# First-layer weights kept as two parts in memory, second-layer weights kept on chip and picked by a register

## Chip, cores and metric

The kernel runs on one core of one Trainium2 chip. The metric is the device time in microseconds (us) of one execution, the median of three.

## What is computed

The reference is one transformer block over `x` of shape (8, 512, 128), all in float32: a linear attention with 16 heads of 64, a residual and a layer norm, then a mixture of 8 experts of which each token takes 2, another residual and a second layer norm. The part that the change is about is the expert part:

```python
logits = einsum('bsd,ed->bse', x, gate_w); probs = softmax(logits)
topk_probs, topk_idx = top_k(probs, 2)
h = gelu(einsum('bsd,fed,bske->bskf', x, w1, onehot) + b1[topk_idx])   # 128 -> 512
y = einsum('bskf,def,bske->bskd', h, w2, onehot) + b2[topk_idx]       # 512 -> 128
x = layernorm(x + sum_k(y * topk_probs))
```

There are 4096 tokens, so 8192 pairs of a token and an expert.

## The kernel before, in words

**Attention.** It runs batch by batch (8 batches `b` of 512 tokens), in `attention(b)` on each engine. TensorE (PE) does keys, queries, a Gram matrix of the inputs with the keys, the norms and the output. Products that need float32 accuracy are made by the helper `three` (L432 to L436): each operand is split into a high part in the type fp32r and the rest, a low part, and three fp32r matmuls are added up. The high part is a copy by ScalarE (ACT, helper `hi`, L666), the low part a subtraction by VectorE (DVE, helper `lo`, L819) or GpSimd (POOL). Near the end of a batch PE runs: half of the queries, two of four tiles of the Gram matrix's first half (`gram(0, (0, 1))`), `norms`, the other two tiles, the second half `gram(1, ...)`, and `mix`. `gram(1)` waits for `n_step` (L563), that is for DVE's instruction of L1116, which reads the norms out of the same PSUM bank. On ACT that place has, in order, the queries' evictions, `first_norm(p)` (L752), the split of the next batch's `xT` (L757) and the eviction of the Gram matrix `gm` (L762). On DVE it has `means` and `scale_logits` (L1111, L1112) and then L1116.

**Experts.** The routed rows are written to a table in memory (`xs`), sorted by expert, and worked off in NBLK = 39 blocks of 256 rows of one expert each, n = 0 to 38. Which expert and which rows a block has is known only at run time; it stands in a table `tabi`, of which the first EARLY = 17 blocks are ready at the end of the attention and the other 22 later (they wait for the last batch's rows). Each engine runs its own list in order:

- SyncE (SP) loads the rows of block n (`load_rows`, L319) and its weights (`load_weights`, L315): it reads the table's entry into a register (`value_load`), and starts a DMA whose address depends on it. One block's weights are one DMA of 578 KB: w1 (128 x 512), b1, w2 (4 x 128 x 128) and b2, 4624 bytes on each of 128 partitions, into one of 6 slots. The loads of block n wait until block n - 6 is finished. Between them SP clears the ends of the experts' regions (`clear_end`, two at each of n = 11 to 14), at n = 17 waits for the last batch's scattered rows (L356 to L360), and from n = 31 on starts the fetches of finished results (`fetch`, L331).
- PE runs, in its iteration n (L651): `turn_rows(n)` (two transposes of the rows), `first_layer(n - 1)` (four float32 matmuls of 256 columns, L639), `second_layer(n - 2)` (eight float32 matmuls of 128 columns, L648). A float32 matmul is two passes in the trace, so that L639 has 8 entries and L648 has 16 in each block.
- ACT copies the transposed rows out of PSUM (L803, L667 in the trace), and does the four gelus with b1 as bias (L794).
- DVE adds b2 (L1136) and scales and adds the rows (L1139) in `result(n - 2)`. After it, in the same list, come the last batch's layer norm and routing (n = 0 to 6), the making of the late table (n = 7 to 11) and, from n = 31 on, statistics of the final layer norm (`last_means`, `last_chain`, at the n of STAT_AT and CHAIN_AT, L57 and L58). `last_means(g)` waits until the fetch of group g has landed.
- POOL scatters the last batch's rows (L395, one piece each at n = 5 to 12) and stores each block's results (L419, two indirect DMAs a block).

What is left of the order: `turn_rows(n)` waits for ACT's copy of the block before (`e_Th`, one PSUM bank up to n = 8, two from then on), and `first_layer(n)` for the copy of its own rows.

```python
for n in range(NBLK + 2):                 # TensorE, L651
    if n < NBLK: turn_rows(n)
    if 1 <= n <= NBLK: first_layer(n - 1)
    if n >= 2: second_layer(n - 2)
```

Of the kernel before, what the change touches and what calls it, by code (L numbers as in the profile page):

```python
# [27 lines left out]
ds = bass.ds  # L28
# [40 lines left out]
KT_SLOTS = 4  # L69
W_ROW = F + FC + FC * D + D  # L70

# [41 lines left out]
def program(nc, x, xT, wqkvT, wf, bf, wout, bout, gwT, w12, consts, out):  # L113
    ctx = ExitStack()
    with ctx:
# [16 lines left out]
        def con(name, rows=P):  # L132
# [5 lines left out]
        wq_hi, wq_lo = sb("wq_hi", [P, HD], F32R), sb("wq_lo", [P, HD], F32R)  # L138
        wk_hi, wk_lo = sb("wk_hi", [P, HD], F32R), sb("wk_lo", [P, HD], F32R)
        vo = sb("vo", [P, H * D])  # L140
        xT_hi, xT_lo = sb("xT_hi", [P, S], F32R), sb("xT_lo", [P, S], F32R)
# [63 lines left out]
        past_l = [qn_space[0:1, a * 704:(a + 1) * 704] for a in range(2)]  # L205
        rows_T = r_rest[:, :]
# [4 lines left out]
        w_raw = [xT_raw[:, u * W_ROW:(u + 1) * W_ROW] for u in range(3)] + [  # L211
            x_raw[:, :, :].rearrange("p c d -> p (c d)")[:, u * W_ROW:(u + 1) * W_ROW] for u in range(SLOTS - 3)]
        w2_raw = [w[:, F + FC:W_ROW - D].rearrange("p (c n) -> p c n", c=FC) for w in w_raw]
        b2_bc = [w[:, None, W_ROW - D:].broadcast_to([P, 2, D]) for w in w_raw]
        x1_space = x1[:, :, :].rearrange("p c d -> p (c d)")
        pair = [space[:, i * TILES * TOPK * D:(i + 1) * TILES * TOPK * D].rearrange("p (t k d) -> p t k d", k=TOPK, d=D)
                for space, i in ((x1_space, 0), (x1_space, 1), (x1_space, 2), (x1_space, 3), (qn_space, 0), (qn_space, 1), (x1_space, 0), (x1_space, 1))]
# [16 lines left out]
        def before(n):  # L234
# [18 lines left out]
        e_x, e_w, e_out = ([sem(f"{n}{u}") for u in range(ROW_SLOTS)] for n in ("e_x", "e_w", "e_out"))  # L253
        e_T, e_Th, e_up, e_gelu, e_down, e_y0, e_y1, e_y = (
            sem(n) for n in ("e_T", "e_Th", "e_up", "e_gelu", "e_down", "e_y0", "e_y1", "e_y"))
        in_xr0, in_fold_q, in_fold_v, tab_step = (sem(n) for n in ("in_xr0", "in_fold_q", "in_fold_v", "tab_step"))
# [35 lines left out]
        def _(sp):  # L292
# [20 lines left out]
            sp.dma_start(xs[NOWHERE:NOWHERE + BLK, :].rearrange("(p f) c -> p f c", p=P), zeros[:, :, :]).then_inc(filled, 16)  # L313

            def load_weights(n):  # L315
                expert = sp.value_load(tabi[0:1, 0, n:n + 1], min_val=0, max_val=E - 1)
                sp.dma_start(w_raw[n % SLOTS], w12[ds(expert, 1), :, :].rearrange("a p n -> (a p) n")).then_inc(e_w[n % SLOTS], 16)

            def load_rows(n):  # L319
                first = sp.value_load(tabi[0:1, 1, n:n + 1], min_val=0, max_val=NOWHERE)  # L320
                sp.dma_start(xrow[n % ROW_SLOTS], xs[ds(first, BLK), :].rearrange("(c p) d -> p c d", p=P)).then_inc(e_x[n % ROW_SLOTS], 16)

            sp.wait_ge(table, 2)
            sp.wait_ge(scattered, 16 * TILES * TOPK * SAFE)
# [104 lines left out]
        def _(pe):  # L429
# [190 lines left out]
            def turn_rows(n):  # L620
                pe.wait_ge(e_x[n % ROW_SLOTS], 16 * (n // ROW_SLOTS) + 16)
                if n == 0:
                    pe.wait_ge(qn_done, CH * B)
                else:
                    pe.wait_ge(e_Th, before(n))
                for c in range(2):
                    last = pe.transpose(psX2[bank_of(n)][:, c * P:(c + 1) * P], xrow[n % ROW_SLOTS][:, c, 0:D], con("ident"))
                last.then_inc(e_T, 1)

            def first_layer(n):  # L630
                v = n % 2
                u = n % SLOTS
                pe.wait_ge(e_Th, n + 1)
                pe.wait_ge(e_w[u], 16 * (n // SLOTS) + 16)
# [6 lines left out]
            def second_layer(n):  # L641
                v = n % 2
                pe.wait_ge(e_gelu, FC * (n + 1))
                if n >= 1:
                    pe.wait_ge(e_y0, before(n))
                for t in range(2):
                    for c in range(FC):
                        last = mm(psY2[bank_of(n)][:, t, :], hT[v][:, c, t * P:(t + 1) * P], w2_raw[n % SLOTS][:, c, :], start=c == 0, stop=c == FC - 1)  # L648
                last.then_inc(e_down, 1)

            for n in range(NBLK + 2):  # L651
                if n < NBLK:
                    turn_rows(n)
                if n == 0:
                    logits(B - 1)
                if 1 <= n <= NBLK:
                    first_layer(n - 1)
                if n >= 2:
                    second_layer(n - 2)
                if n == 6:  # L660
                    ranks(B - 1)
# [3 lines left out]
        def _(act):  # L665
# [30 lines left out]
            def first_norm(p):  # L696
                act.wait_ge(ln_step, LN_STEPS * (p + 1))
                for j in range(TILES):
# [88 lines left out]
            def gelu(n):  # L787
                v, u = n % 2, n % SLOTS
                act.wait_ge(e_w[u], 16 * (n // SLOTS) + 16)
                for c in range(FC):  # L790
                    act.wait_ge(e_up, FC * n + c // 2 * 2 + 2)
                    if c == 0 and n >= 2:
                        act.wait_ge(e_down, n - 1)
                    act.activation(hT[v][:, c, :], psH[v][:, c, :], ACT.Gelu_apprx_tanh,  # L794
                                   bias=w_raw[u][:, F + c:F + c + 1]).then_inc(e_gelu, 1)

            for n in range(NBLK + 1):
                if n < NBLK:
# [3 lines left out]
                    v = n % 2  # L802
                    hi(rows_T[:, v * BLK:(v + 1) * BLK], psX2[bank_of(n)], scale=2.0).then_inc(e_Th, 1)  # L803
                if n >= 1:
# [13 lines left out]
        def _(dve):  # L818
# [227 lines left out]
            def attention(b):  # L1046
# [172 lines left out]
```

## Time and profile before

| what | value |
|---|---|
| three executions | 472.32, 473.69, 474.63 us; median 473.69 |
| the profiled execution | 474.31 us, of which the span from first to last instruction is 472.5 |
| busy: PE, DVE, ACT, POOL | 437.2, 300.6, 273.1, 162.2 us |
| mean granted PE clock | 0.983 |

Columns of the rows below: in the timeline, start and length in us, engine, line of the kernel, operation, out<-in by the program's names, shape, xcount, and in brackets the engine's idle time just before and what ended it. PEld is PE's weight load, SPq an instruction in SP's own queue. The names are those of the memory: the weights' slots lie in `xT_raw` and `x_raw`, the blocks' rows in `kT` and `rn`, the hidden layer and the results in `q_act`, the final groups in `x` and `qn`. Entries of the same kind that follow each other are merged into one row, and its length is then that of them all, overlaps and drain included.

### The profile page before, as it was taken

How to read it: one execution, taken by the hardware profiler on the slowest of the kernel's cores; microseconds unless marked ns; L12 is line 12 of the kernel's file. 1: busy time of each engine (PE TensorE's matmuls, PEld its weight loads, DVE VectorE, ACT ScalarE, POOL GpSimd, SP SyncE). 2: the span in 40 equal slices, each digit the busy share in tenths (PEclk: the TensorE clock that was granted, in tenths of full speed). 3: DMA queues.
4: the chain of work that ended last, by engine and by line, in shares of the span. 5: the costliest groups of instructions: out<-in, count | busy, mean ns of one | idle time of the engine just before them, and what ended most of it. 6: DMA issues, size and time to landing. Idle time of an engine off the chain costs nothing.

```text
span 472.5 us, 8134 instructions
## 1 busy us (share of the span) xinstructions
PE 437.2 (93%) x2608; PEld 343.4 (73%) x2608; DVE 300.6 (64%) x896; ACT 273.1 (58%) x531; POOL 162.2 (34%) x164
## 2 busy tenths in 40 slices
PE   4888999999999999999999998799999999999940
PEld 4666776676677677667677674499998999999930
DVE  2654865976976967967967967743563222245784
ACT  2763655665666665665666562278555555555672
POOL 2101101131332233233143133165777545555540
PEclk9999999999999999999999999999999999999995
DMA  8920000000000000000000000598895998799343
GB/s 222 336 70 0 3 0 1 0 19 6 26 23 1 25 23 1 23 25 6 19 24 13 12 25 23 171 318 234 235 276 167 321 286 238 232 337 311 122 134 112
DMA packets 34442, 52.19 MB, mean 110 GB/s; under 512 B 4943, under 2 KB 24788, under 8 KB 34272
## 3 DMA queue, kind: packets, MB, share of 16 engines
q1 hardware_dynamic: 25296, 40.75, 28.4%
q0 software_dynamic: 4544, 8.54, 5.1%
q10 hardware_dynamic: 4560, 2.39, 1.7%
q8 instruction: 21, 0.34, 0.3%
q14 instruction: 21, 0.17, 0.1%
HBM read 39.82 MB, written 12.75 MB: 111 GB/s over the span
## 4 chain that ended last, share of the span: by engine, by line
PE 82%; DVE 6%; DMA 4%; issue 3%; SPq 2%; POOL 2%; ACT 1%; POOLq 0%; DVEq 0%; ACTq 0%
PE psA L639 13%; PE psO L531 11%; PE psG L648 8%; PE psA L434 6%; PE psA L436 6%; PE psA L435 6%; PE psA L510 6%; PE psS L648 5%; PE psG L434 4%; PE psG L551 3%; PE psG L435 3%; PE psG L436 3%; PE psA L578 3%; PE psG L522 3%; DMA x_raw<-x 1%
## 5 line engine op out<-in xcount | busy, mean ns | idle before, releaser
L395 POOL DMA_INDIRECT expert_rows<-rows,pos x64 | 62.5, 977 | 116.7 <-DVE pos L1025 91.1
L419 POOL DMA_INDIRECT expert_results<-q_act,kT x56 | 55.3, 987 | 41.6 <-DVE q_act L1139 30.5
L531 PE MATMUL psO<-qn,mixed 128*128 128x512 f32 x128 | 65.8, 599 | 0.4 <-DVE qn L1056 0.4
L667 ACT ACTIVATE kT<-psA,bf_col 128x512 f32<-128x512 f32 x64 | 44.0, 687 | 37.0 <-PE psA L436 36.7
L667 ACT ACTIVATE q_act<-psA,bf_col 128x512 f32<-128x512 f32 x64 | 43.9, 690 | 26.4 <-PE psA L436 26.3
L1056 DVE TENSOR_TENSOR qn<-q_act,psG 128x512 f32<-128x512 f32 x64 | 43.0, 681 | 5.0 <-PE psG L522 5.0
L820 DVE TENSOR_TENSOR k_lo<-psA,k_hi 128x512 fp32r<-128x512 f32 x64 | 43.7, 686 | 3.5 <-ACT k_hi L667 2.8
L510 PEld LDWEIGHTS psA<-cst,kT 128*128 128x128 f32 x256 | 30.8, 140 | 16.2 <-ACT kT L667 8.3
L794 ACT ACTIVATE q_act<-psA,xT_raw 128x256 f32<-128x256 f32 x84 | 34.6, 471 | 11.8 <-PE psA L639 11.1
L639 PE MATMUL psA<-r_rest,xT_raw 128*128 128x256 f32 x168 | 41.3, 391 | 0.0
L434 PE MATMUL psA<-xT_hi,wk_hi 128*128 128x512 f32 x64 | 41.0, 641 | 0.0
L510 PE MATMUL psA<-cst,kT 128*128 128x128 f32 x256 | 38.7, 274 | 2.4 <-DVE k_lo L820 1.4
L667 ACT ACTIVATE k_hi<-psA 128x512 fp32r<-128x512 f32 x64 | 38.1, 596 | 2.0 <-PE psA L510 2.0
L1068 DVE TENSOR_REDUCE ksum<-kT 128x2 f32<-128x1024 f32 x32 | 38.7, 1210 | 0.0
L794 ACT ACTIVATE q_act<-psA,x_raw 128x256 f32<-128x256 f32 x72 | 29.7, 471 | 8.4 <-PE psA L639 8.0
L639 PE MATMUL psA<-r_rest,x_raw 128*128 128x256 f32 x144 | 34.1, 379 | 0.0
L639 PEld LDWEIGHTS psA<-r_rest,xT_raw 128*128 128x128 f32 x168 | 31.2, 196 | 3.6
L648 PEld LDWEIGHTS psG<-xT_raw,q_act 128*128 128x128 f32 x256 | 31.0, 192 | 1.4 <-ACT q_act L794 0.6
L386 POOL TENSOR_TENSOR xT_lo<-xT_raw,xT_hi 128x512 fp32r<-128x512 f32 x8 | 10.3, 1284 | 63.3 <-ACT xT_hi L667 63.3
L648 PE MATMUL psG<-xT_raw,q_act 128*128 128x128 f32 x256 | 31.3, 275 | 0.4 <-ACT q_act L794 0.4
L386 POOL TENSOR_TENSOR x_lo<-x_raw,x_hi 128x512 fp32r<-128x512 f32 x8 | 10.3, 1292 | 59.5 <-ACT x_hi L667 59.5
L667 ACT ACTIVATE gm<-psG 128x512 f32<-128x512 f32 x16 | 9.6, 597 | 34.1 <-PE psG L436 34.1
(180 smaller groups left out, 915.8 us busy)
## 6 DMA issues: line engine op xcount, KB each, us to landing
xT_raw<-w SPq DMA_DIRECT2D x21, 578.0 KB, 4.7
x_raw<-w SPq DMA_DIRECT2D x18, 578.0 KB
kT<-expert_rows SPq DMA_DIRECT2D x28, 132.0 KB, 4.6
x<-expert_results SPq DMA_DIRECT2D x5, 512.0 KB, 6.4
xT_raw<-xT SPq DMA_DIRECT2D x1, 1792.0 KB, 10.4
q_act<-wqkvT SPq DMA_DIRECT2D x3, 512.0 KB, 6.9
rn<-expert_rows SPq DMA_DIRECT2D x11, 132.0 KB, 3.7
out<-x ACTq DMA_DIRECT2D x5, 256.0 KB, 2.3
```

The source lines that it names most:

```text
L395: pool.indirect_dma_start(xs, bass.IndirectOffsetOnAxis(ap=pos[:, j, k:k + 1], axis=0), rows[:, j, k, :], None).then_inc(scattered if o < ...
L419: pool.indirect_dma_start(ys, bass.IndirectOffsetOnAxis(ap=xrow[r][:, c, D:D + 1].bitcast(I32), axis=0), yrow[u][:, c, :], None, bounds_ch ...
L434: mm(outp, a_hi, b_hi, start=start, stop=False)
L435: mm(outp, a_hi, b_lo, start=False, stop=False)
L510: last = pe.transpose(bankA[2 + c % 2][:, at], kT[:, (CH * b + c) % KT_SLOTS, at], con("ident"))
L531: mm(psO[:, :], mixed[:, c, :], qn[:, c % 4, :], start=c == 0, stop=c == CH - 1).then_inc(o_pe, 1)
L639: mm(psH[v][:, c, :], w_raw[u][:, c * P:(c + 1) * P], rows_T[:, at], start=True, stop=True).then_inc(e_up, 1)
L648: last = mm(psY2[bank_of(n)][:, t, :], hT[v][:, c, t * P:(t + 1) * P], w2_raw[n % SLOTS][:, c, :], start=c == 0, stop=c == FC - 1)
L667: return act.activation(out_, in_, func, **kw)
L794: act.activation(hT[v][:, c, :], psH[v][:, c, :], ACT.Gelu_apprx_tanh, bias=w_raw[u][:, F + c:F + c + 1]).then_inc(e_gelu, 1)
L820: return dve.tensor_tensor(out_, full_, hi_.bitcast(F32), ALU.subtract)
L1056: dve.tensor_tensor(qn[:, c % 4, :], q_act[:, c, :], psG[:, c % 2, :], ALU.mult).then_inc(qn_done, 1)
```

## The change

The first layer is made by `three` instead of by float32 matmuls: 12 fp32r matmuls of 256 columns a block instead of 4 float32 ones. For this w1 is split once for each of the 8 experts, during attention batches 1 to 4 (two experts each, `SPLIT_AT`), by ACT and DVE, and written back to memory as `w1s` (high and low part side by side). SP loads w1's two parts for each block (512 KB) and b1 and b2 by two small DMAs. w2 of all experts is loaded once (2 MB) and stays on chip; PE reads the block's expert into a register (`choose`) and the matmuls of the second layer take w2 at an address that depends on it. The rows' low part is a new instruction of DVE at the head of each iteration, and PE waits for it (`e_Tl`) where it waited for ACT's copy (`e_Th`).

```diff
-W_ROW = F + FC + FC * D + D
+W_ROW = FC + D
+W1_SLOTS = 8
+SPLIT_AT = {1: (0, 1), 2: (2, 3), 3: (4, 5), 4: (6, 7)}
...
+        w1s = nc.dram_tensor("expert_weights", [E, P, 2 * F], F32, kind="Internal").ap()
...
+            for half in range(2):
+                if half:
+                    sp.wait_ge(w1_l, E // 2)
+                sp.dma_start(w1_raw, w12[4 * half:4 * half + 4, :, 0:F].rearrange("e p f -> p e f")).then_inc(in_w1[half], 16)
+                for ex in range(4 * half, 4 * half + 4):
+                    sp.wait_ge(w1_l, ex + 1)
+                    sp.dma_start(w1s[ex, :, :], w1_split[ex % 2][:, :].bitcast(F32)).then_inc(w1_out[ex % 2], 16)
+            sp.wait_ge(x_l, B)
+            sp.wait_ge(x_h, B)
+            sp.dma_start(w2_all.rearrange("p (e n) -> p e n", e=E), w12[:, :, F + FC:F + FC + FC * D].rearrange("e p n -> p e n")).then_inc(w2_in, 16)
...
             def load_weights(n):
                 expert = sp.value_load(tabi[0:1, 0, n:n + 1], min_val=0, max_val=E - 1)
-                sp.dma_start(w_raw[n % SLOTS], w12[ds(expert, 1), :, :].rearrange("a p n -> (a p) n")).then_inc(e_w[n % SLOTS], 16)
+                sp.dma_start(w1_slot[n % W1_SLOTS].bitcast(F32), w1s[ds(expert, 1), :, :].rearrange("a p n -> (a p) n")).then_inc(e_w[n % W1_SLOTS], 16)
+                for cols, part in ((slice(0, FC), slice(F, F + FC)), (slice(FC, W_ROW), slice(F + FC + FC * D, F + FC + FC * D + D))):
+                    sp.dma_start(b_raw[n % SLOTS][:, cols], w12[ds(expert, 1), :, part].rearrange("a p n -> (a p) n")).then_inc(e_b[n % SLOTS], 16)
...
# TensorE, turn_rows: waits for e_Tl, not e_Th
+            def choose(n):
+                if n == 0:
+                    pe.wait_ge(w2_in, 16)
+                if n in (0, EARLY):
+                    pe.wait_ge(table, 2 if n == 0 else 4)
+                return pe.value_load(tabi[0:1, 0, n:n + 1], min_val=0, max_val=E - 1)
...
             def first_layer(n):
-                pe.wait_ge(e_Th, n + 1)
+                pe.wait_ge(e_Tl, n + 1)
                 for c in range(FC):
-                    mm(psH[v][:, c, :], w_raw[u][:, c * P:(c + 1) * P], rows_T[:, at], start=True, stop=True).then_inc(e_up, 1)
+                    three(psH[v][:, c, :], w1_slot[u][:, c * P:(c + 1) * P], w1_slot[u][:, F + c * P:F + (c + 1) * P],
+                          xT_hi[:, at], xT_lo[:, at]).then_inc(e_up, 1)
...
             def second_layer(n, expert):
-                        last = mm(psY2[bank_of(n)][:, t, :], hT[v][:, c, t * P:(t + 1) * P], w2_raw[n % SLOTS][:, c, :], ...)
+                        last = mm(psY2[bank_of(n)][:, t, :], hT[v][:, c, t * P:(t + 1) * P], w2_all[:, ds(expert * (FC * D) + c * D, D)], ...)
...
             for n in range(NBLK + 2):
                 if n >= 2:
-                    second_layer(n - 2)
+                    second_layer(n - 2, expert)
+                if 1 <= n <= NBLK:
+                    expert = choose(n - 1)
...
# ScalarE, attention(b), after the split of the next xT and before gm
+                    for ex in SPLIT_AT.get(b, ()):
+                        act.wait_ge(in_w1[ex // 4], 16)
+                        if ex >= 2:
+                            act.wait_ge(w1_out[ex % 2], 16 * (ex // 2))
+                        hi(w1_split[ex % 2][:, 0:F], w1_raw[:, ex % 4, :]).then_inc(w1_h, 1)
...
# VectorE, attention(b), after scale_logits and before L1116
+                for ex in SPLIT_AT.get(b, ()):
+                    dve.wait_ge(w1_h, ex + 1)
+                    lo(w1_split[ex % 2][:, F:], w1_raw[:, ex % 4, :], w1_split[ex % 2][:, 0:F]).then_inc(w1_l, 1)
...
# VectorE, experts, at the head of iteration n
+                if n < NBLK:
+                    at = slice(n % 2 * BLK, (n % 2 + 1) * BLK)
+                    dve.wait_ge(e_Th, n + 1)
+                    dve.scalar_tensor_tensor(xT_lo[:, at], psX2[bank_of(n)], 2.0, xT_hi[:, at].bitcast(F32), ALU.mult, ALU.subtract).then_inc(e_Tl, 1)
```

## Rows read from the trace of the kernel before

**Rows 1.** The page: busy time, and DMA busy share in 40 slices.

```profile
PE 437.2 (93%) x2608; PEld 343.4 (73%) x2608; DVE 300.6 (64%) x896; ACT 273.1 (58%) x531; POOL 162.2 (34%) x164
...
DMA  8920000000000000000000000598895998799343
```

**Rows 2.** The page: the chain that ended last, shares of the span by line.

```profile
PE psA L639 13%; PE psO L531 11%; PE psG L648 8%; PE psA L434 6%; PE psA L436 6%; PE psA L435 6%; PE psA L510 6%; PE psS L648 5%; PE psG L434 4%; PE psG L551 3%; PE psG L435 3%; PE psG L436 3%; PE psA L578 3%; PE psG L522 3%; DMA x_raw<-x 1%
```

**Rows 3.** Timeline of one block of the steady expert stretch.

```profile
377.06 0.38 PE L627 MATMUL psG<-cst,kT 128*128 128x128 f32 x2
...
377.26 0.42 DVE L1136 TENSOR_TENSOR q_act<-psS,x_raw 128x256 f32<-128x256 f32 x1 [2.66 <-PE psS L648]
377.28 1.89 PE L639 MATMUL psA<-r_rest,xT_raw 128*128 128x256 f32 x8
...
377.72 0.61 DVE L1139 SCALAR_TENSOR_TENSOR q_act<-q_act,rn 128x128 f32<-128x128 f32 x2
...
379.01 1.95 PE L648 MATMUL psG<-xT_raw,q_act 128*128 128x128 f32 x16
...
380.79 0.38 PE L627 MATMUL psO<-cst,kT 128*128 128x128 f32 x2
```

**Rows 4.** Timeline of attention batch 1, around L1116 and the Gram matrix.

```profile
73.53 0.64 ACT L667 ACTIVATE xT_hi<-xT_raw 128x512 fp32r<-128x512 f32 x1
...
74.24 1.28 POOL L386 TENSOR_TENSOR xT_lo<-xT_raw,xT_hi 128x512 fp32r<-128x512 f32 x1 [24.43 <-ACT xT_hi L667]
...
74.35 0.69 DVE L1116 TENSOR_SCALAR rn<-psG 128x512 f32<-128x512 f32 x1 [2.02 <-PE psG L551]
...
75.50 0.39 PE L436 MATMUL psG<-k_hi,x_lo 128*128 128x512 f32 x1
...
75.72 0.39 PE L434 MATMUL psG<-k_hi,x_hi 128*128 128x512 f32 x1
...
75.92 0.60 ACT L667 ACTIVATE gm<-psG 128x512 f32<-128x512 f32 x1 [1.76 <-PE psG L436]
```

**Rows 5.** Groups of instructions (busy us, mean ns | idle before): the nearest to the new splits.

```profile
L820 DVE TENSOR_TENSOR k_lo<-psA,k_hi 128x512 fp32r<-128x512 f32 x64 | 43.7, 686 | 3.5 <-ACT k_hi L667 2.8
...
L1146 DVE TENSOR_TENSOR x<-x 128x512 f32<-128x512 f32 x4 | 2.7, 685 | 0.0
```

**Rows 6.** SP's queue at the start of the experts; the page's DMA issues.

```profile
302.09 0.34 SPq L317 DMA_DIRECT2D xT_raw<-w  x1
...
304.35 0.34 SPq L317 DMA_DIRECT2D xT_raw<-w  x1
...
xT_raw<-w SPq DMA_DIRECT2D x21, 578.0 KB, 4.7
```

**Rows 7.** Instructions of L316 on SP (ns min/median/max): a register load.

```profile
L316 SPq TENSOR_LOAD <-tabi x39: 262/274/563, 299.1 to 434.4; - x39
L316 SPq FUSED_REGOPS  x39: 152/152/165, 299.4 to 434.7; - x39
```

**Rows 8.** Timeline of SP's queue with two clears between loads.

```profile
330.83 1.55 SPq L341 DMA_DIRECT2D expert_rows<-zeros  x2
...
333.15 0.41 SPq L321 DMA_DIRECT2D kT<-expert_rows  x1
```

**Rows 9.** Timeline around block 17: its row load and PE's first use.

```profile
363.47 0.38 SPq L321 DMA_DIRECT2D rn<-expert_rows  x1
...
365.81 0.44 PE L627 MATMUL psO<-cst,rn 128*128 128x128 f32 x2 [0.45 <-DMA rn<-expert_rows]
```

**Rows 10.** Timeline of the late stretch: statistics on DVE, and one fetch.

```profile
423.03 0.68 DVE L1146 TENSOR_TENSOR x<-x 128x512 f32<-128x512 f32 x1
...
424.73 0.38 DVE L1153 BATCH_NORM_AGGREGATE mv<-stats 128x2 f32<-128x6 f32 x4
...
432.66 0.33 SPq L336 DMA_DIRECT2D qn<-expert_results  x1
...
437.96 0.69 DVE L1146 TENSOR_TENSOR x<-x 128x512 f32<-128x512 f32 x1
```

More of the change, by code:

```diff
@@ L139, in program @@
         wk_hi, wk_lo = sb("wk_hi", [P, HD], F32R), sb("wk_lo", [P, HD], F32R)
+        w1_split = [sb(f"w1_split{i}", [P, 2 * F], F32R) for i in range(2)]
         vo = sb("vo", [P, H * D])
@@ L210, in program @@
                 for space, fit in ((kT_space, 7), (rn_space, ROW_SLOTS - 7)) for u in range(fit)]
[L211 to L214, printed above, removed]
+        b_raw = [xT_raw[:, u * W_ROW:(u + 1) * W_ROW] for u in range(SLOTS)]
+        b2_bc = [b[:, None, FC:].broadcast_to([P, 2, D]) for b in b_raw]
+        w1_slot = [space[:, u, :] for space in (k_hi, k_lo) for u in range(W1_SLOTS // 2)]
+        w2_all = x_raw[:, :, :].rearrange("p c d -> p (c d)")
         x1_space = x1[:, :, :].rearrange("p c d -> p (c d)")
+        w1_raw = x1_space[:, 4 * F:8 * F].rearrange("p (e f) -> p e f", f=F)
         pair = [space[:, i * TILES * TOPK * D:(i + 1) * TILES * TOPK * D].rearrange("p (t k d) -> p t k d", k=TOPK, d=D)
@@ L253, in program @@
         e_x, e_w, e_out = ([sem(f"{n}{u}") for u in range(ROW_SLOTS)] for n in ("e_x", "e_w", "e_out"))
-        e_T, e_Th, e_up, e_gelu, e_down, e_y0, e_y1, e_y = (
-            sem(n) for n in ("e_T", "e_Th", "e_up", "e_gelu", "e_down", "e_y0", "e_y1", "e_y"))
+        e_T, e_Th, e_Tl, e_up, e_gelu, e_down, e_y0, e_y1, e_y = (
+            sem(n) for n in ("e_T", "e_Th", "e_Tl", "e_up", "e_gelu", "e_down", "e_y0", "e_y1", "e_y"))
+        in_w1 = [sem(f"in_w1_{i}") for i in range(2)]
+        w1_h, w1_l, w2_in = (sem(n) for n in ("w1_h", "w1_l", "w2_in"))
+        w1_out = [sem(f"w1_out{i}") for i in range(2)]
+        e_b = [sem(f"e_b{u}") for u in range(SLOTS)]
         in_xr0, in_fold_q, in_fold_v, tab_step = (sem(n) for n in ("in_xr0", "in_fold_q", "in_fold_v", "tab_step"))
@@ L321, in load_rows @@
                 sp.dma_start(xrow[n % ROW_SLOTS], xs[ds(first, BLK), :].rearrange("(c p) d -> p c d", p=P)).then_inc(e_x[n % ROW_SLOTS], 16)
+            for which in w1_out:
+                sp.wait_ge(which, 16 * E // 2)
             sp.wait_ge(table, 2)
@@ L624, in turn_rows @@
                 else:
-                    pe.wait_ge(e_Th, before(n))
+                    pe.wait_ge(e_Tl, before(n))
                 for c in range(2):
@@ L628, in turn_rows @@
                 last.then_inc(e_T, 1)
+            def choose(n):
[4 more added lines that the diff above has]
+                return pe.value_load(tabi[0:1, 0, n:n + 1], min_val=0, max_val=E - 1)
             def first_layer(n):
-                v = n % 2
-                u = n % SLOTS
-                pe.wait_ge(e_Th, n + 1)
-                pe.wait_ge(e_w[u], 16 * (n // SLOTS) + 16)
+                v, u = n % 2, n % W1_SLOTS
+                pe.wait_ge(e_w[u], 16 * (n // W1_SLOTS) + 16)
+                pe.wait_ge(e_Tl, n + 1)
                 if n >= 2:
@@ L638, in first_layer, with second_layer @@
                 for c in range(FC):
-                    mm(psH[v][:, c, :], w_raw[u][:, c * P:(c + 1) * P], rows_T[:, at], start=True, stop=True).then_inc(e_up, 1)
-            def second_layer(n):
+                    three(psH[v][:, c, :], w1_slot[u][:, c * P:(c + 1) * P], w1_slot[u][:, F + c * P:F + (c + 1) * P],
+                          xT_hi[:, at], xT_lo[:, at]).then_inc(e_up, 1)
+            def second_layer(n, expert):
                 v = n % 2
@@ L647, in second_layer @@
                     for c in range(FC):
-                        last = mm(psY2[bank_of(n)][:, t, :], hT[v][:, c, t * P:(t + 1) * P], w2_raw[n % SLOTS][:, c, :], start=c == 0, stop=c == FC - 1)
+                        last = mm(psY2[bank_of(n)][:, t, :], hT[v][:, c, t * P:(t + 1) * P], w2_all[:, ds(expert * (FC * D) + c * D, D)], start=c == 0, stop=c == FC - 1)
                 last.then_inc(e_down, 1)
@@ L697, in first_norm @@
                 act.wait_ge(ln_step, LN_STEPS * (p + 1))
+                if p == 4:
+                    act.wait_ge(w1_l, E)
                 for j in range(TILES):
@@ L788, in gelu @@
                 v, u = n % 2, n % SLOTS
-                act.wait_ge(e_w[u], 16 * (n // SLOTS) + 16)
+                act.wait_ge(e_b[u], 32 * (n // SLOTS) + 32)
                 for c in range(FC):
@@ L802, in _ @@
                     v = n % 2
-                    hi(rows_T[:, v * BLK:(v + 1) * BLK], psX2[bank_of(n)], scale=2.0).then_inc(e_Th, 1)
+                    hi(xT_hi[:, v * BLK:(v + 1) * BLK], psX2[bank_of(n)], scale=2.0).then_inc(e_Th, 1)
                 if n >= 1:
```

3 lines of the change are left out of this document (1 added, 2 removed).

## The prediction

> **What bounds the kernel now.** I began with the page: PE is busy 93% of the span, the others 64% or less [rows 1], and the chain that ended last runs through PE's lines in both stages, L639 and L648 in the experts and L531 and L434 to L436 in the attention [rows 2]. So a pass saved on PE is time saved, unless something else is close behind it. The timeline of one block shows how close. PE's period is 3.73 us (377.06 to 380.79): 0.22 for the transposes, 1.73 for the first layer's eight passes, 1.78 for the second layer's sixteen [rows 3]. In that time DVE needs 1.07 us for a block's result (377.26 to 378.33) and then waits for PE. DMA engines are busy 0.7 to 0.9 in most of the expert stage [rows 1]; the bytes per block stay the same (578 KB), so I leave them at nothing, with the prefetch of several blocks as cover. The close one is SP, which is not on the chain: its loads for a block follow each other at 2.26 us when it waits for nothing [rows 6].
>
> **First layer on PE.** Removed: 8 passes of 256 columns, 1.73 us. Added: 12 fp32r passes of 256 columns. The nearest rows are fp32r passes of 512 columns, 0.22 to 0.23 us apart (75.50 to 75.72) [rows 4]; half is 0.115. The weight load must fit under a pass: in L648 a load and a pass come every 0.111 us (1.78 / 16) [rows 3], so 0.115 is not below what it allows. Lower end 0.111; upper end 0.23, if an fp32r load could not be hidden under a shorter pass. I take 0.115, as L648's pace is the nearer row: 1.38 us, a saving of 0.35, and a PE period of 3.38 us.
>
> **SP.** A block now has four DMAs instead of two. A pair of register load and DMA costs 1.13 us (2.26 / 2). The two new DMAs use a register that is already loaded. Each costs at least its own 0.34 [rows 6], and at most 1.13 less the load (0.274) and the register operation (0.152) of rows 7, about 0.7. I take 0.52, the middle, as both ends are the same instruction with and without its address work. SP's period becomes 2.26 + 1.04 = 3.30 us (2.94 to 3.66), beside PE's 3.38: nothing is left to catch up with. Where SP has more to do, PE now waits. That is at the clears of n = 11 to 14, at 2.3 us for each pair (330.83 to 333.15) [rows 8], 9.2 us in all.
>
> **The early blocks, up to block 17.** Before, the weights of block 1 are issued at 302.09 [rows 6]. Now it is about 303.1 (block 0's two small DMAs precede them), so those of block 16 go out at 303.1 + 15 x 3.30 + 9.2 = 361.8 and land 4.7 later [rows 6], at 366.5. Block 16's rows are one SP step earlier (about 360.7) and arrive near 364 to 365; with block 15's first layer and block 14's second behind their transposes (3.4 us) PE reaches block 17 at about 367.4, not at 365.81 [rows 9]. Block 17's own rows are no earlier either: they were issued at 363.47, after the scatter [rows 9], and SP gets there at about 364. The whole early gain (17 x 0.35 = 6 us) is lost and **1.6 us** are added. If SP's step were 2.94, this would be 17 x 0.35 less what the scatter's chain holds back, some 2 us gained; at 3.66, 7 us lost.
>
> **The late blocks, 17 to 38.** 21 periods x 0.35 = **-7.3 us**. Against it stands DVE. The new low part of block n + 1 is at the head of DVE's iteration, behind whatever the iteration before left, and PE's first layer waits for it; before, PE waited only for ACT. Its price: 128x256 from PSUM, as L1136, 0.42 [rows 3], 0.46 with its gap. From n = 31 on a statistics iteration costs 2.1 us (423.03 to 425.11) [rows 10] besides the result's 1.07: with the 0.46 together 3.63, above 3.38. Three such iterations in a row cost 0.8; the norm chain and the next ones about as much again. The fetch issued at 432.66 was used at 437.96 [rows 10], 5.3 us later with no wait. Now two more small DMAs precede its issue (1.04) and four blocks between come 4 x 0.35 sooner, so DVE waits some 2.4 us at n = 37 with block 38's low part behind it, part of which the queues absorb. Together I give back **3.0 us** (1 to 5). The tail after the last transposes has one first layer in it, **-0.3**.
>
> **Attention, batches 1 to 4.** Two splits each on ACT, 0.64 us like xT_hi [rows 4], and two subtractions on DVE, 0.69 each [rows 5]. On ACT they fit: it stood idle 1.76 us before gm, and takes 1.3. On DVE they do not. ACT is free at 74.17, the splits end at 74.8 and 75.5, the second subtraction at about 76.2, and only then comes L1116, which ran at 74.35: 1.85 us late, done at 76.9. gram(1) waits for it, and its first pass started at 75.72 [rows 4]: PE stands 1.2 us, 1.35 with the wake-up. POOL and SP have nothing behind it. Later in the batch DVE's reciprocal and the norms shift by as much as PE, so it is not paid twice. 4 x 1.35 = **+5.4 us** (0, if PE had slack that I do not see, to 7). The stores of w1s and w2's load run while DMA is idle [rows 1] and cost nothing.
>
> By a rule of the Trainium skill (SBUF — State Buffer, Who interferes with whom) a VectorE instruction with two SBUF inputs contends with a GpSimd instruction that reads SBUF. The new subtractions are of that kind.
>
> The trace has such an instruction of DVE only where POOL does no arithmetic (L1146, 685 ns) [rows 5]. POOL's xT_lo runs from 74.24 to 75.52 [rows 4], over the first subtraction's start at 74.9. If it must wait, 0.65 us a batch are added.
>
> **Register on PE.** `choose` costs PE's own queue a load and a register operation, 0.43 us by SP's [rows 7], and each of 8 matmuls may need address work. The queue runs ahead of the array, so I put it at nothing; the cover is the work queued in front. Not hidden, it would be 0.43 and more a block.
>
> **Sum.** 5.4 + 1.6 - 7.3 + 3.0 - 0.3 = +2.4, or 2.5 with the small DMAs at the start. On the profiled execution (474.31, span 472.5 and 1.8 around it) that is 476.8; it lies 0.6 above the median, so for the median 473.7 + 2.5 = **476.2 us**.
>
> **Rivals.** A measurement of this kernel tells 0.5% (2.4 us) from no change: below 471.3 is faster, above 476.1 slower.
>
> *A, the forecast.* Own range 471 to 480. Chance 0.42 (0.04 faster, 0.20 same, 0.18 slower).
>
> *B, the saving comes through.* It decides at SP's new DMAs: at 0.4 or less each its step is below 3.1 and PE keeps its own pace. Early -2, late -7.3 + 2, tail -0.3, attention +4: -3.6, 470.1. For it: both added DMAs skip the register load. Against it: address work remains. Chance 0.28 (0.26 faster).
>
> *C, SP sets the pace.* At 0.7 each its step is 3.66. Early +7, late 21 x (3.66 - 3.73) = -1.5, the fetches' own time on SP +1.5, attention +5.4: +12.4, 486. Chance 0.10.
>
> *D, three passes cost what two did or more.* Passes of 0.144 make the saving zero, and the sum without its -7.3 and without most of the 3.0 is 481; at 0.23 a block is 1.03 longer, 473.7 + 5.4 + 39 x 1.03 = 519. Against it is L648's pace. Chance 0.02. That is also the case in which the change doesn't do what it says.
>
> *E, PE's queue does not run ahead.* Register load (0.43) and the address work of 8 matmuls (0.05 each at the least) then show in each block, 0.8 us, 0.45 more than the saving: 473.7 + 5.4 + 39 x 0.45 = 497. Nothing in the trace shows a matmul with such an address. Chance 0.10.
>
> *F, the subtractions wait for POOL.* 4 x 0.65 = 2.6 on top: 478.8. Chance 0.08, as no row shows it. By the rule of the Trainium skill named above it would be certain.
>
> **How the numbers follow.** The forecast is A's. The range 467.5 to 486 takes in A, B, C and F with SP's and DVE's bounds, and leaves out D, E and the thin ends, 0.2. Faster 0.26 + 0.04 = 0.30; same 0.20 + 0.02 = 0.22; slower 0.18 + 0.10 + 0.02 + 0.10 + 0.08 = 0.48.
>
> **What the changed profile would show.** Right: L434 to L436 with 256 columns every 0.115 us; L1116 about 1.9 us later against the norms and PE idle 1.3 us before gram(1) in batches 1 to 4; four SP DMAs a block, 3.3 us apart, and PE waiting for `expert_rows` loads around blocks 12 to 17; block 17 at or after 366 plus the attention's 5; a late pace of 3.38 with waits of PE for DVE's low part from n = 31 on. Wrong: an SP step under 3.1, no PE idle at gram(1), or PE idle in every block between second layer and transposes, which would be the register.

## The result, and the profile after

The changed kernel takes **489.12 us** (median of 4, 487.52 to 493.09) where the kernel before takes 474.16 (472.32 to 474.96) on the same chip: 1.034 times as long, 95% interval 1.030 to 1.039. The forecast was 476.2 with a range to 486. The profiled execution has a span of 485.8 us, 13.3 over the 472.5 of before. Seven of the eighteen runs below fell on chips where the kernel before itself takes 490 to 491 us, so each is read by its ratio to the kernel before beside it; most of those seven were made again on a chip where that takes 475, but not `e6_pool_after` and `s3_before_pieces`. A ratio leaves out executions more than 1.5% above the fastest of the same kernel, which are two of `e1_split_later` alone. Brackets behind a ratio are its 95% interval.

I cut both traces at the same places: the start of the first expert block's transposes, of block 17's, and of block 38's, the last. Below, a period of PE is the time from one block's first transpose to the next one's, and a step of SP the time from the issue of one block's rows to that of the next.

| stretch | before | after | difference | forecast |
|---|---|---|---|---|
| to block 0 (the attention) | 302.1 | 309.4 | +7.3 | +5.4 |
| block 0 to 17 | 63.7 | 70.1 | +6.4 | +1.6 |
| block 17 to 38 | 78.4 | 79.6 | +1.2 | -4.3 |
| block 38 to the end | 28.3 | 26.7 | -1.6 | -0.3 |
| sum | 472.5 | 485.8 | +13.3 | +2.4 |

The page after, parts 1, 2 and 4 (they answer to [rows 1, 2]):

```profile
PE 434.1 (89%) x2764; PEld 345.0 (71%) x2764; DVE 322.2 (66%) x943; ACT 275.0 (57%) x539; POOL 162.0 (33%) x164
...
PE   4979998998998998999999998799968999979950
...
PE 56%; SPq 15%; DVE 11%; issue 7%; DMA 6%; ACT 3%; POOL 1%; POOLq 0%; DVEq 0%; ACTq 0%
PE psO L554 10%; PE psA L457 6%; PE psA L459 6%; PE psA L458 6%; PE psA L533 5%; SPq L338 4%; PE psA L601 3%; PE psG L457 3%; PE psG L545 3%; PE psG L679 2%; SPq L341 2%; PE psG L458 2%; PE psG L459 2%; PE psS L679 2%; SPq L342 2%
```

PE's busy time fell by only 3 us, although 39 first layers are shorter, in part because some of it ran at half clock (below). And SP's queue, with 2% of the chain before, now holds 15% of it, with the two small DMAs (L338) as its largest line. What PE waited for (us in total, times, longest):

```profile
PE psG L650 <- DMA kT<-expert_rows: 7.8, 5, 2.3
PE psG L457 <- DVE rn L1159: 6.1, 4, 1.6
PE psO L650 <- DMA kT<-expert_rows: 3.7, 3, 2.5
...
PE psG L650 <- DMA rn<-expert_rows: 0.7, 1, 0.7
```

Two waits have come up: for the row loads that SP issues (12.2 us in nine; before, one of 0.5 us at block 17), and for DVE's L1159 (none for L1116, as it was before). The timeline of a late block, which answers to [rows 3]; where PE starts late, the row names what released it:

```profile
389.87 0.38 PE L650 MATMUL psG<-cst,kT 128*128 128x128 f32 x2
...
390.05 1.46 SPq L342 DMA_DIRECT2D kT<-expert_rows  x1
...
390.45 0.28 PE L457 MATMUL psA<-xT_hi,k_hi 128*128 128x256 f32 x1
...
390.56 0.28 PE L458 MATMUL psA<-xT_lo,k_hi 128*128 128x256 f32 x1
...
391.06 0.41 DVE L1208 SCALAR_TENSOR_TENSOR xT_lo<-psG,xT_hi 128x256 fp32r<-128x256 f32 x1
...
391.52 1.95 PE L679 MATMUL psG<-x_raw,q_act 128*128 x16
...
392.27 0.33 SPq L336 DMA_DIRECT2D k_lo<-expert_weights  x1
392.80 0.85 SPq L338 DMA_DIRECT2D xT_raw<-w  x2
...
394.43 0.33 PE L650 MATMUL psO<-cst,kT 128*128 128x128 f32 x1 [0.96 <-DMA kT<-expert_rows]
```

The passes are 0.12 us apart and the two layers follow each other without a gap: PE's period is 3.43 us where nothing is late. Here something is: one SP issue (L342) took 1.46 us instead of 0.38, and PE stands 0.96 us at the rows of the block after. SP's queue over the clears, which answers to [rows 8]:

```profile
345.10 1.57 SPq L364 DMA_DIRECT2D expert_rows<-zeros  x2
347.50 0.41 SPq L342 DMA_DIRECT2D kT<-expert_rows  x1
348.83 0.35 SPq L336 DMA_DIRECT2D k_hi<-expert_weights  x1
349.38 0.85 SPq L338 DMA_DIRECT2D xT_raw<-w  x2
350.99 1.47 SPq L364 DMA_DIRECT2D expert_rows<-zeros  x2
353.21 0.41 SPq L342 DMA_DIRECT2D kT<-expert_rows  x1
```

A step with clears takes 5.71 us (347.50 to 353.21), and PE's blocks 11 to 14 are 5.93, 6.12, 5.76 and 5.03 us apart. In the attention, batch 1, which answers to [rows 4]:

```profile
73.75 1.16 ACT L700 ACTIVATE w_split<-x 128x512 fp32r<-128x512 f32 x2
...
73.95 1.29 POOL L409 TENSOR_TENSOR xT_lo<-xT_raw,xT_hi 128x512 fp32r<-128x512 f32 x1 [24.42 <-ACT xT_hi L700]
...
74.42 1.96 DVE L860 TENSOR_TENSOR w_split<-x,w_split 128x512 fp32r<-128x512 f32 x2 [2.39 <-ACT w_split L700]
...
76.31 0.68 DVE L1159 TENSOR_SCALAR rn<-psG 128x512 f32<-128x512 f32 x1
...
77.04 0.50 PE L457 MATMUL psG<-k_hi,x_hi 128*128 128x512 f32 x1 [1.44 <-DVE rn L1159]
```

The two subtractions take 1.96 us together, L1159 starts at 76.31 where L1116 did at 74.35, and PE's second Gram half at 77.04 instead of 75.72. The batch itself began 0.28 us earlier here (PE's first key matmul at 45.95, before at 46.23), so that within the batch L1159 is 2.24 us later. Last, three stretches of the experts (us; busy time and instructions of each engine, then granted clock, DMA share, GB/s):

```profile
313.30:320.10 6.80, 6.07 (x30) 5.78 (x29) 3.84 (x22) 3.82 (x10) 5.26 (x6) 0.50 0.93 241
368.00:371.40 3.40, 3.40 (x19) 3.40 (x17) 0.42 (x1) 2.03 (x5) 2.33 (x3) 0.50 0.80 246
436.20:439.60 3.40, 3.40 (x19) 3.40 (x18) 1.15 (x7) 1.87 (x5) 1.27 (x2) 0.50 0.96 289
```

The granted clock is 0.50, the lower level of 1.2 GHz, for 13.6 us; in the kernel before for only 3.4 us between its first and its last expert block (305.8 to 309.2). The last two stretches follow waits of PE for rows.

### The profile page after: what moved, and what is told of

It is laid out like the page before. It is cut to its first block, busy times and chain, and to the rows that moved or that the text cites. A ratio compares the mean times of both kernels' runs of the same rounds, so it can differ in the third digit from the quotient of the medians.

```text
span 485.8 us, 9037 instructions
## 1 busy us (share of the span) xinstructions
PE 434.1 (89%) x2764; PEld 345.0 (71%) x2764; DVE 322.2 (66%) x943; ACT 275.0 (57%) x539; POOL 162.0 (33%) x164
## 4 chain that ended last, share of the span: by engine, by line
PE 56%; SPq 15%; DVE 11%; issue 7%; DMA 6%; ACT 3%; POOL 1%; POOLq 0%; DVEq 0%; ACTq 0%
PE psO L554 10%; PE psA L457 6%; PE psA L459 6%; PE psA L458 6%; PE psA L533 5%; SPq L338 4%; PE psA L601 3%; PE psG L457 3%; PE psG L545 3%; PE psG L679 2%; SPq L341 2%; PE psG L458 2%; PE psG L459 2%; PE psS L679 2%; SPq L342 2%
## 5 line engine op out<-in xcount | busy, mean ns | idle before, releaser
L834 ACT ACTIVATE q_act<-psA,xT_raw 128x256 f32<-128x256 f32 x156 | 61.7, 476 | 17.5 <-PE psA L459 17.2
L679 PE MATMUL psG<-x_raw,q_act 128*128 x384 | 48.7, 281 | 0.2 <-ACT q_act L834 0.2
L679 PEld LDWEIGHTS psG<-x_raw,q_act 128*128 128x128 f32 x384 | 47.0, 199 | 0.5 <-issue 0.4
L1179 DVE TENSOR_TENSOR q_act<-psG,xT_raw 128x256 f32<-128x256 f32 x24 | 10.2, 424 | 38.9 <-PE psG L679 38.6
L457 PE MATMUL psG<-k_hi,x_hi 128*128 128x512 f32 x64 | 26.4, 413 | 7.9 <-DVE rn L1159 6.1
L409 POOL TENSOR_TENSOR x_lo<-x_raw,x_hi 128x512 fp32r<-128x512 f32 x8 | 10.4, 1295 | 66.6 <-ACT x_hi L700 66.6
L409 POOL TENSOR_TENSOR xT_lo<-xT_raw,xT_hi 128x512 fp32r<-128x512 f32 x8 | 10.3, 1287 | 63.1 <-ACT xT_hi L700 63.1
L679 PE MATMUL psS<-x_raw,q_act 128*128 x240 | 29.2, 275 | 0.0
L457 PE MATMUL psA<-xT_hi,wq_hi 128*128 128x512 f32 x64 | 28.5, 446 | 0.0
```

Source lines behind the costliest of these rows:

```text
L457: mm(outp, a_hi, b_hi, start=start, stop=False)
```

## The experiments

In kernels with more lines the same instruction has a higher number: L650 of the changed kernel is L655 in e2, e3, r2 and r4, and L633 in r3.

**My theory:** (a) the subtractions stand in front of L1159 and make PE wait, more than forecast because POOL holds them up; (b) SP's step with two more issues leaves no lead over PE, so its clears, fetches and long issues reach PE. **Rivals:** the low part on DVE, PE's own passes or the register set the experts' pace; or it is memory traffic and not issue time.

### The subtractions on DVE

`e1_split_later`:

```
-                for ex in SPLIT_AT.get(b, ()):  (ahead of L1159)
+                    (the same three lines behind the reciprocals of L1163)
```

> Edit: the two subtractions of w1's low parts are taken from in front of DVE's L1159 (the norms) and put behind the two reciprocals of L1163, where DVE waits some 1.9 us a batch for ACT. Theory (the subtractions delay L1159, and PE's second Gram half waits for it, 4 x 1.84 us, the stall of 1.9 to 2.0 us seen in batches 1 to 4): all of the 7.3 us of the attention come back, batch periods of 34.2 to 34.5 us, about 481.8 us. Rival (the splits cost through ACT, POOL or DMA, wherever DVE does its part): at most 2 us come back, over 487.

Measured: 485.67 us (478.46 to 487.03), 1.015 [1.004, 1.026], the ratio from 478.46 and 485.44 alone. DVE in batch 1:

```profile
74.75 0.69 DVE L1156 TENSOR_SCALAR rn<-psG 128x512 f32<-128x512 f32 x1 [2.03 <-PE psG L574]
75.48 3.37 DVE L1160 RECIPROCAL rn<-rn 128x256 f32<-128x256 f32 x2
...
78.76 1.22 DVE L860 TENSOR_TENSOR w_split<-x,w_split 128x512 fp32r<-128x512 f32 x2
```

Both subtractions take 1.22 us with POOL done, PE's wait for L1159 is gone, and the periods of batches 1 to 4 (from PE's first key matmul to that of the next batch) are 34.22, 34.53, 34.53 and 34.83 (before 34.22, 34.51, 34.56, 34.53; after 35.93, 36.25, 36.40, 36.68). So the attention's loss is this one place: block 0 starts at 303.0 instead of 309.4. The total doesn't follow, though: the profiled run, of 485.90 us, took 153.2 us from block 0 to 38 instead of 149.6, with 9 SP issues over half a microsecond, 8.4 us of excess. The runs lie 8.6 us apart. That the rest of the 7.3 us is lost in SP's queue is likely, not shown by this run alone; between e2 and e3 below, where SP has two DMAs a block, the same edit gives 6.9 us.

`e6_pool_after` (POOL's L409 in batches 1 to 4):

```
                 pool.wait_ge(xT_h, b + 2)
+                if b in SPLIT_AT:
+                    pool.wait_ge(w1_l, SPLIT_AT[b][-1] + 1)
```

> Edit: in batches 1 to 4 POOL's xT_lo waits until DVE has done both subtractions of w1. Theory (the first subtraction takes 1.3 us instead of 0.68 because POOL reads memory at the same time): both subtractions 0.68 us, L1159 0.6 us earlier, 4 x 0.6 = 2.4 us less in the attention, batch periods of 35.4 to 36.0 us, 486.5 us in all. Rival (the first of the two is slow by itself, by its form or ACT's write just before it): still 1.3 us, and no change or slightly slower.

Measured: 508.28 us on a chip where the kernel before takes 489.95, 1.040 [1.033, 1.047]; the total says nothing without the changed kernel beside it, but the attention's periods can be read: the kernels that have the changed kernel's attention agree in them to 0.1 us on all chips. All eight subtractions (ns min/median/max), and batch 1:

```profile
L862 DVE TENSOR_TENSOR w_split<-x,w_split x8: 684/689/694, 75.9 to 183.9; 128x512 fp32r<-128x512 f32 x8
```
```profile
75.92 1.29 DVE L862 TENSOR_TENSOR w_split<-x,w_split 128x512 fp32r<-128x512 f32 x2 [2.39 <-ACT w_split L702]
...
77.36 1.28 POOL L409 TENSOR_TENSOR xT_lo<-xT_raw,xT_hi 128x512 fp32r<-128x512 f32 x1 [26.35 <-DVE w_split L862]
```

In the changed kernel the same row read 676/1020/1375. Periods of 35.29, 35.55, 35.78 and 36.04, 2.6 us less in all. The contention is shown: a subtraction that starts under POOL's takes 1.3 us (1.96 less 0.68 in batch 1; 1.36 to 1.38 by its own record in each of the four batches, 0.69 here), and POOL itself loses nothing (1.29 and 1.28 us).

### SP's two small DMAs

`e2_one_load`:

```
+W1_ROW = 2 * F + W_ROW          (b1 and b2 stored beside w1's two parts)
-                for cols, part in (...): sp.dma_start(b_raw[...])
-        w1_slot: 8 of 2 * F columns
+        w1_slot: 6 of W1_ROW columns, b_raw = w[:, 2 * F:]
```

> Edit: the biases are stored beside w1's two parts in memory, so that one DMA brings 1156 columns a block where three DMAs did; six slots of weights instead of eight. Theory (SP's step of 3.3 us and its lack of a lead cost the early and the late blocks): SP step 2.26 us, waits of PE for expert_rows gone or under 2 us in all, the span from the first transposes to the last 13 to 14 us shorter (early 8, late 5 to 6), about 475.5 us. Rival (DVE's low part and the clock set the experts' pace, SP only follows): less than 4 us come back, over 485.

Measured: 476.11 us (473.67 to 478.13), 1.001 [0.998, 1.004]. As expected, SP's step is 2.26; block 0 to 38 took 134.7 us instead of 149.6. One long wait of PE for rows is left, 2.6 us behind block 16, where SP waits 8.5 us for POOL's scatter of the last batch; all such waits together are 4.0 us, where under 2 was expected. Not expected: the first batch ended 4.1 us later (its last products began at 48.2, not 44.1). I put it down to the biases' loads, which stand in front of other work in the queue at the start; but single profiles of kernels without them show late first batches too (50.9 in r3), so it isn't shown.

`e7_before_small` and again `r3_before_small`, the kernel before with the loads alone:

```
+                for cols, part in (...): sp.dma_start(spare[:, n % SLOTS, cols], w12[...])
```

> The kernel before, with two small DMAs of the biases added behind each block's weights (into a tile that nothing reads), and nothing else of the change. Theory (SP's added issues cost by themselves): SP's step from 2.26 to 3.3 us and more with long issues among them, early blocks 3 to 6 us later, late ones 0 to 2, about 479 us (476 to 483). Rival (the small DMAs only hurt together with a shorter PE period): within 1.5 us of the kernel before.

> As e7_before_small (the kernel before, with two small DMAs of the biases added to each block's loads). On the slower chip it was 1.3% over the kernel before. Theory (SP's added issues cost by themselves, about 6 us through the early blocks): 1.006 to 1.018 times the kernel before. Rival (they only hurt together with PE's shorter period): within 1.5 us of the kernel before.

Measured: 495.97 beside 489.95, 1.013 [1.008, 1.019]; and 481.64 beside 475.62, 1.012 [1.009, 1.015]. Two of its SP steps:

```profile
346.52 0.41 SPq L327 DMA_DIRECT2D kT<-expert_rows  x1
347.70 0.35 SPq L319 DMA_DIRECT2D x_raw<-w  x1
348.23 0.85 SPq L323 DMA_DIRECT2D spare<-w  x2
349.84 1.47 SPq L347 DMA_DIRECT2D expert_rows<-zeros  x2
352.14 0.41 SPq L327 DMA_DIRECT2D kT<-expert_rows  x1
```

A step with clears is 5.62 us. From block 0 to 17 it took 70.4 us (63.7 before), from 17 to 38 78.4, as before: the issues alone give the whole early loss, even at PE's old period of 3.73, and no late one.

`e5_two_passes` and again `r2_two_passes`, which leave one pass in three out of the first layer:

```
-                    three(psH[v][:, c, :], ...)
+                    two(psH[v][:, c, :], ...)
```

> Left out: the pass of the first layer with w1's high and the rows' low part, so that PE has eight passes of 256 columns a block instead of twelve, 0.48 us less (39 x 0.48 = 18.7 us in all); everything that SP does stays. Theory (SP, whose step is 3.3 us and more, sets the pace of the changed kernel's experts): at most 4 us of it are seen, 485 us or more, steps of SP unchanged and more waits of PE for expert_rows. Rival (PE's passes still set the pace, and SP's waits are single events): 15 us or more, 474 or less.

> As e5_two_passes (left out: the pass with w1's high and the rows' low part; 18.7 us less of PE's passes). Theory (SP's step sets the experts' pace): at most 4 us less than r1_after. Rival (PE's passes set it): 15 us or more less.

Beside them `r1_after`, the changed kernel: 

> The changed kernel as it is, as the measure for the three beside it: the last four ran on a chip where the kernel before itself took 490 us, so they are read here again, against both kernels on one chip. Theory and rivals: about 1.034 times the kernel before where that takes 474 us; on the slower chip more, since its long instruction gaps and issues come in the experts' stage, where the changed kernel has no lead.

Measured: e5 510.68 beside 489.95, 1.042 [1.037, 1.047]; then r2 486.80, 1.023 [1.020, 1.025], beside r1's 490.09, 1.029 [1.024, 1.035]. Of 18.7 us of passes 3.3 came through. What PE waited for in r2:

```profile
PE psG L655 <- DMA kT<-expert_rows: 13.7, 10, 3.5
...
PE psO L655 <- DMA kT<-expert_rows: 6.8, 7, 2.3
...
PE psG L655 <- DMA rn<-expert_rows: 2.8, 3, 1.5
```

PE only waits longer (23.3 us for rows, 14.6 in r1). A faster PE is of little use here; SP sets the pace.

`s1_one_row` and again `t1_one_row` (issues kept, packets gone), `s2_one_small` and again `t2_one_small` (the second bias's load left out), with `t3_after`, the changed kernel:

```
-   b_raw[n % SLOTS][:, cols], w12[ds(expert, 1), :, part]        (both loads)
+   b_raw[n % SLOTS][0:1, cols], w12[ds(expert, 1), 0:1, part]    (s1, t1)
+   for cols, part in ((slice(0, FC), slice(F, F + FC)),):        (s2, t2)
```

> Left out: the biases of 127 of 128 partitions; each of the two small DMAs moves one row instead of 128, so their issues stay on SP and their packets go. Theory (the issues' own time on SP is the loss): SP's step stays 3.3 us, 485 to 489 us. Rival (their many small packets hold up the queue and the other loads): 476 or less. The long issues of 1 us and more, 7 to 10 in the changed kernel, tell how much of it is the packets': if these make them, they go, and 3 to 5 us with them.

> Left out: the load of the second bias, so that one small DMA stands in each block's loads; SP's step should be 2.78 us, 0.65 below PE's 3.43, enough to catch up with the four steps of clears. Theory (what counts is whether SP's step with its clears and fetches leaves a lead over PE, so the loss has a threshold): nearly all of what e2_one_load gave comes back with half of the issues, 473 to 477 us. Rival (each issue costs its share, as on a shared path): half of it, 482 us or more.

> As s1_one_row (left out: the biases of 127 of 128 partitions; the issues stay, their packets go), now beside the changed kernel on one chip. Theory (the issues' time on SP is the loss): within 4 us of t3_after, SP's step 3.3 us. Rival (the packets hold up the loads): 8 us or more below t3_after.

> As s2_one_small (left out: the second bias's load; one small DMA a block, SP's step 2.78 us). Theory (a threshold in SP's lead): 11 to 14 us below t3_after, close to e2_one_load. Rival (in proportion to the issues): 5 to 8 us below it.

> The changed kernel as it is, the measure for the two beside it. Theory and rivals: 1.03 times the kernel before where that takes 475 us, 1.04 or more on a chip where that takes 490, as the gaps there leave SP further behind.

Measured: s1 511.68 and s2 502.50 beside 490.87, 1.043 [1.035, 1.051] and 1.022 [1.015, 1.029], with no changed kernel on that chip. Then t3 489.49, 1.032 [1.027, 1.037]; t1 489.24, 1.032 [1.026, 1.039]; t2 478.77, 1.008 [1.006, 1.010]. With one row instead of 128 nothing is gained in the total. The instructions of L338 and of the register load L341 (ns min/median/max), t1 first, then t3:

```profile
L338 SPq DMA_DIRECT2D xT_raw<-w x78: 228/260/298, 307.9 to 456.0; - x78
```
```profile
L341 SPq TENSOR_LOAD <-tabi x39: 263/511/671, 305.2 to 452.9; - x39
```
```profile
L338 SPq DMA_DIRECT2D xT_raw<-w x78: 332/333/1472, 309.7 to 457.7; - x78
```
```profile
L341 SPq TENSOR_LOAD <-tabi x39: 262/270/493, 306.1 to 454.8; - x39
```

The long issues did go (t1 has one over half a microsecond, t3 ten), but the register load behind them took 0.51 us instead of 0.27, so that SP's step was 3.45 us in place of 3.30 with some at 4 and more: the gain of 3 to 5 us that I had expected from them didn't come. Why the register load is slower I can't say. As SP's step grew by 0.15 us with it, the run shows that the issues alone, without the packets, suffice for the whole loss; it doesn't show that the packets cost nothing. The other question: one small DMA fewer gave 0.0244 of 475, 11.6 us (10.7 between the medians, just short of the 11 expected), where taking both away gave 14 to 15 between blocks 0 and 38 (e2). Some four fifths come with half the issues, which speaks for a threshold: at 2.78 us SP catches up with PE's 3.43 after the clears (PE's periods there are 3.43 to 3.49 but for one of 4.34), at 3.30 it does not (5.03 to 6.12 in the changed kernel).

### The register

`e4_no_register`:

```
-                return pe.value_load(tabi[0:1, 0, n:n + 1], min_val=0, max_val=E - 1)
+                return 0        (and w2_all[:, c * D:(c + 1) * D])
```

> Left out: the choice of the second layer's weights by expert; all blocks take those of expert 0 at a constant address, with no register load on PE. Theory (PE's queue hides the register and the address work): within 1 us of the changed kernel, 488 to 490. Rival (the register costs PE's queue time in each block, 0.45 us or more): 470 or less.

Measured: 489.29 us, 1.031 [1.026, 1.037], the same as with the register. Where SP sets the pace the total alone could hide a cost on PE; PE's period is 3.43 us in both where nothing is late, so the register costs nothing that can be seen.

### Both repairs, and more

`e3_both` is e1 and e2 together.

> Both edits, that of the splits and that of the single load. Theory: the two losses are in different stages and add up, 489 - 7.3 - 13.5 = about 468 us, 6 below the kernel before. Rival (a common cause, such as contention in memory): well above that, 474 or more.

Measured: 469.21 us (468.09 to 472.44), 0.987 [0.982, 0.992]. The two losses are separate and add up. Left were the late first batch and the wait behind block 16 (intervals of 6.46 and 5.03 us). `e8_better` and again `r4_better` take these too:

```
 (the biases' loads into the store now behind the stores of w1)
-                if 5 <= n < 5 + PIECES:
-                    scatter(B - 1, (n - 5,))
+                if 5 <= n < 5 + PIECES // 2:
+                    scatter(B - 1, (2 * (n - 5), 2 * (n - 5) + 1))
```

> Both repairs (subtractions behind the reciprocals, one load a block), and two more: the biases' loads into the store are issued after the batches have begun instead of ahead of them, where they made the first batch 3.5 us longer, and POOL scatters the last batch's rows two pieces a block, so that SP's wait of 8.6 us for them ends sooner. Theory: 469.2 - 3.5 - about 4 (the two intervals of 6.5 and 5.0 us behind block 16 back to 3.43, less some of DVE's) = 461 to 463 us. Rival (the scatter's wait only hides the clears' backlog of SP, and the first batch's delay was slack): above 466.

> As e8_better (subtractions behind the reciprocals, one load a block, the biases' loads later, two pieces of the last batch's rows a block). On the slower chip its attention was 3.6 us shorter than e3_both's, and the wait behind block 16 was gone, but the experts had gaps of 5 to 11 us which no semaphore explains. Theory (those gaps were the chip's): 0.97 to 0.98 times the kernel before, and 6 to 8 us below e3_both's 469 where the kernel before takes 475. Rival (the edits themselves make the gaps, POOL's two pieces a block in front of its stores): above 0.987 times the kernel before.

Measured: e8 497.86 beside 489.95, 1.017 [1.012, 1.023]; r4 **465.51 us** (464.19 to 469.93) beside 475.62, **0.981** [0.975, 0.987]. Its chain, by engine, and two of its blocks (L655 are the transposes):

```profile
PE 86%; DVE 5%; DMA 3%; SPq 2%; issue 1%; ACT 1%; POOL 0%; POOLq 0%; DVEq 0%; ACTq 0%
```
```profile
382.97 0.38 PE L655 MATMUL psO<-cst,kT 128*128 128x128 f32 x2
...
386.40 0.38 PE L655 MATMUL psG<-cst,kT 128*128 128x128 f32 x2
```

PE waits for no row load, and every late interval is 3.41 to 3.44 up to the last five. Block 0 to 17 took 58.8 us, 17 to 38 72.7. The gain over e3 is 3.7 us between the medians, not the 6 to 8 that I expected, and the ratio stands just outside 0.97 to 0.98; neither the theory nor its rival (over 0.987) has it. On the slower chip the same kernel lost all of this again.

`s3_before_pieces` gives the scatter's edit to the kernel before.

> The kernel before with one edit of r4_better's alone: POOL scatters the last batch's rows two pieces a block. Theory (the kernel before is bound by PE at 3.73 us a block and waits for these rows only 0.6 us, once, so r4_better's gain is that of the split weights): at most 1 us less than the kernel before, ratio 0.998 to 1.002. Rival (the earlier scatter by itself is worth some 5 us): 471 or less where the kernel before takes 475.

Measured: 489.88 beside 490.87, 0.998 [0.995, 1.001]. So the scatter's edit by itself gives nothing, and r4's gain is most likely that of the split weights once SP and DVE are kept out of the way. This was measured on a slower chip only, where r4's kernel gained nothing either (e8).

## Why the prediction was wrong

**SP, the step that failed.** The prediction took 3.30 us for SP's step "beside PE's 3.38: nothing is left to catch up with". The plain step is 3.30 to the hundredth, and each added DMA costs its 0.52. But I let every step take that. Outside the clears the steps to block 16 took 3.50 on average, and a step with clears 5.7 to 6.4 instead of 5.6. Two things are in that which the sum left out: long issues (0.5 to 1.7 us, ten of 174 in the whole stage, four of them by block 16, with 1.3 us of excess) and long register loads (up to 0.57 us, 1.9 us of excess by block 16), of which [rows 7] had shown one, 0.56 beside a median of 0.27. In r1 and t3 it was more the issues, 2.2 and 3.5 us, and less the loads, 0.7 in each. The kernel before has both too (three long issues of 94), but its step of 2.26 leaves room for them. SP issued block 16's rows 66.3 us after block 0's, not 62.0 (16 x 3.30 + 9.2): 4.3 of the 4.8 us by which the early term was too small. r3 shows that term alone, +6.6.

**The late term.** -7.3 + 3.0 was forecast, +1.2 came (-0.4 in r1, -0.6 in t3). The give-back was put in the wrong place. DVE's low part with the statistics costs little: r4, where SP is out of the way, took 72.7 us for 21 x 3.43 = 72.0, so 0.7 and not 3.0. Instead SP, at 3.52 on average from block 17 to 31 and 4.0 to 4.8 in the steps with a fetch, held PE back by 5 to 7 us. Rival C (chance 0.10) had this mechanism and its 486 came nearest, but I made it hang on a price of 0.7 us a DMA. It came true at 0.52: a mean step above PE's period is enough. That its sum lies near the result is in part luck, as the price was not the reason.

**PE.** 0.12 us a pass and 3.43 a block, for 0.115 and 3.38: 39 x 0.05 = 2.0 us, a small miss. Rival D is out by that pace, rival E by e4. Rival B is out by its own condition: the new DMAs cost 0.52 each, not 0.4 or less.

**The attention.** The mechanism and its place were right. Without POOL in the way (e6) the four batches cost 1.07, 1.04, 1.22 and 1.51 us, 4.8 in all, for the 5.4 forecast. The rest, 2.6 us, is rival F, just the 0.65 a batch that it was priced at. That it fits so closely is in part luck: it was priced with a start 0.62 us before POOL's end (74.9 and 75.52), and the subtraction starts 0.82 before it (74.42 and 75.24). I gave it 0.08 because no row showed it. F alone made 478.8, so it doesn't explain the result by itself. The Trainium skill (SBUF — State Buffer, Who interferes with whom) says that a VectorE instruction with two SBUF inputs contends with a GpSimd instruction that reads SBUF, and the traces agree: 1.3 us for a subtraction that starts under POOL's, 0.68 without. It should have stood in the forecast.

**The clock** I had not priced. Besides the stretch in the periods of blocks 1 and 2 (313.3 to 320.1), two periods fell to 1.2 GHz after waits for rows (5.03 and 5.05 us instead of 3.43). Whether these 3.2 us reach the end while SP sets the pace was not tried by itself. The tail was 1.3 us shorter than forecast (0.7 and 0.8 in r1 and t3); the cause of that stays open.

## What to carry to other kernels

A period that is 8% shorter on the bound engine can be worth nothing if the change gives the queue that feeds it more issues: add up the mean step of that queue with its rare work and its long issues, and ask for a clear margin under the new period; a step just below it is not enough. Two small DMAs a block cost more here than the 0.30 us a block that PE gained; with their data stored beside the large one's, and the other repairs, a loss of 3% became a gain of 2%. And put side work on an engine into its own idle time (behind the reciprocals), not merely near it, in front of what another engine waits for.

## What was not expected of the hardware

- SP's DMA issues are sometimes long: on the chips where the kernel before takes 475, five to ten of 174 took 0.5 to 1.7 us with four a block, two or three of some 95 with two a block. With one-row transfers one of 174 did, but the register load that followed took 0.51 us instead of 0.27. What makes them long stays open.
- Chips differ for this program: the kernel before took 475 us on some and 490 on others. The attention's periods are the same; the experts have gaps there, inside a layer and without a semaphore. From e8's timeline, a first layer whose passes should be 0.12 us apart:

```profile
340.45 0.37 PE L462 MATMUL psA<-xT_hi,k_hi 128*128 128x256 f32 x1 [0.15 <-issue]
341.89 0.36 PE L463 MATMUL psA<-xT_lo,k_hi 128*128 128x256 f32 x1 [1.07 <-issue]
...
343.28 0.28 PE L464 MATMUL psA<-xT_hi,k_hi 128*128 128x256 f32 x1 [1.04 <-issue]
```

  In the kernel before with s3's edit the periods before blocks 4 and 10 took 9.4 and 10.4 us. What holds the engine there stays open. It doesn't go by the number of DMAs: with four a block the kernel before stands at 1.013 there and 1.012 here (e7, r3), while e8 with two a block stands at 1.017 there and 0.981 here (r4).
